# A fused cross-attention and FFN kernel: later FFN weight loads, a new order on every engine, filler products in the fill, rope pairs in fours

## The reference

```python
x = x + xattn(layernorm(x), ctx, pos)        # x: 16 batches x 128 tokens x 256
x = x + ffn(layernorm(x))
# xattn: q = x@Wq, k, v = split(ctx@Wkv); 32 heads of 8 values
#   rope on q and k: per head 2 positions x 2 frequencies x (x1, x2)
#   out = (x1*cos - x2*sin, x1*sin + x2*cos)
#   softmax(q k^T / sqrt(8)) v, then @Wout + bout
# ffn: 4-bit fake-quantised x, W1 (1024x256), W2 (256x1024); relu, h clipped to 0..15
#   the weight scale is max|W| / 7, so W1 and W2 are needed whole before they are rounded
```

## Time and profile before

| what | value |
|---|---|
| median of 3 runs | 263.78 us (262.29 to 264.59) |
| the profiled execution, its own time | 261.2 us |
| its span, first to last instruction | 259.2 us |
| PE busy | 219.5 us (85%) |
| DVE busy | 202.3 us (78%) |
| ACT busy | 183.8 us (71%) |
| POOL busy | 145.2 us (56%) |
| DMA | 11.28 MB, mean 44 GB/s |

### The profile page before, as it was taken

The page is one execution under the profiler, slowest core; times in us unless marked ns, Lnnn a source line. Parts: engine busy times, 40 slices in busy tenths (PEclk is TensorE's granted clock), DMA queues, the critical chain, the costliest instruction groups (busy, mean ns, idle before and its releaser), DMA issues.

```text
span 259.2 us, 8209 instructions
## 1 busy us (share of the span) xinstructions
PE 219.5 (85%) x3126; PEld 173.6 (67%) x3126; DVE 202.3 (78%) x418; ACT 183.8 (71%) x346; POOL 145.2 (56%) x232
## 2 busy tenths in 40 slices
PE   0342775897899999999999999999999999899763
PEld 0142663765677878788877887878787778687541
DVE  5188449967559898989898998989898989884641
ACT  2132339675557979788897979797979799788553
POOL 3158747583636675858493949494948381411320
PEclk9999957599689999999999999999999999999985
DMA  7982000029000000100010001000100010010101
GB/s 193 369 243 89 0 3 1 4 51 359 4 4 4 1 4 4 44 6 5 1 46 4 4 5 44 3 4 4 44 4 5 3 46 5 4 44 4 42 0 40
DMA packets 11381, 11.28 MB, mean 44 GB/s; under 512 B 3920, under 2 KB 10576, under 8 KB 11216
## 3 DMA queue, kind: packets, MB, share of 16 engines
q1 hardware_dynamic: 8864, 10.23, 12.1%
q10 hardware_dynamic: 2480, 0.54, 1.0%
HBM read 8.41 MB, written 2.10 MB: 41 GB/s over the span
## 4 chain that ended last, share of the span: by engine, by line
PE 72%; POOL 6%; DVE 6%; DMA 6%; issue 6%; ACT 3%; ACTq 0%; POOLq 0%; DVEq 0%
PE ps_misc L947 43%; PE ps_av L947 14%; PE ps_exp L947 12%; PE ps_max L947 4%; DMA wq<-in_L_xattn_Wq_dram 3%; DMA q_stack<-mxT 3%; ACT h_i L606 2%; POOL rot L444 2%; DVE mx L797 1%; POOL qk_rows L455 1%; POOL xcT_hi L431 1%; POOL v_strip L395 1%; POOL xcT_lo L434 1%; DVE xq_i L854 1%; POOL v_strip L469 1%
## 5 line engine op out<-in xcount | busy, mean ns | idle before, releaser
L797 DVE TENSOR_REDUCE mx<-ps_max 128x8 f32<-128x1024 f32 x64 | 78.0, 1219 | 14.5 <-PE ps_max L947 12.6
L576 ACT ACTIVATE expo<-ps_exp 128x1024 f32<-128x1024 f32 x64 | 68.3, 1068 | 7.9 <-PE ps_exp L947 7.8
L444 POOL TENSOR_TENSOR rot<-by_cos,by_sin 128x256 f32<-128x256 f32 x32 | 26.3, 842 | 54.2 <-DVE by_sin L787 54.2
L606 ACT ACTIVATE h_i<-ps_misc,b1q,relu_scale 128x128 int16<-128x128 f32 x128 | 49.2, 499 | 1.3 <-PE ps_misc L947 1.2
L947 PE MATMUL ps_exp<-q_stack,k_stack 25*128 25x128 f32 x512 | 44.0, 290 | 5.6 <-DMA q_stack<-mxT 3.0
L947 PE MATMUL ps_misc<-ident,qk_rows 128*128 128x128 f32 x256 | 40.0, 293 | 9.0 <-POOL qk_rows L455 9.0
L947 PEld LDWEIGHTS ps_exp<-q_stack,k_stack 25*128 25x128 f32 x512 | 34.9, 191 | 16.9 <-issue 8.7
L947 PE MATMUL ps_av<-expo,v_strip 128*32 128x128 f32 x1024 | 42.3, 285 | 0.0
L947 PEld LDWEIGHTS ps_misc<-ident,qk_rows 128*128 128x128 f32 x256 | 32.0, 152 | 11.0 <-issue 6.0
L947 PEld LDWEIGHTS ps_av<-expo,v_strip 128*32 128x32 f32 x1024 | 24.8, 111 | 6.9 <-issue 0.8
L866 DVE TENSOR_SCALAR hq<-h_i 128x512 bf16<-128x512 int16 x32 | 18.7, 586 | 11.9 <-ACT h_i L606 11.9
(11 more groups left out here) (117 smaller groups left out, 447.7 us busy)
## 6 DMA issues: line engine op xcount, KB each, us to landing
w<-in_L_ffn_W_dram SPq DMA_DIRECT2D x2, 1024.0 KB, 8.1
out_dram<-y SPq DMA_DIRECT2D x8, 256.0 KB, 2.8
xcT<-in_ctx_dram SPq DMA_DIRECT2D x1, 1536.0 KB, 6.5
x_all<-in_x_dram SPq DMA_DIRECT2D x1, 1024.0 KB, 10.5
xcT<-in_ctx_dram SPq DMA_DIRECT2D x1, 768.0 KB, 6.6
x_all<-in_x_dram SPq DMA_DIRECT2D x1, 512.0 KB, 7.6
q_stack<-mxT SPq DMA_DIRECT2D x32, 8.0 KB
xcT<-in_ctx_dram SPq DMA_DIRECT2D x2, 192.0 KB, 3.5
```

Source lines behind the costliest of these rows:

```text
L444: pool.tensor_tensor(out[:, :, c], kept[:, :, c], turned[:, :, 1 - c], ALU.add).then_inc(rot_ready, 1)
L576: act.activation(expo[:, at, :], ps_exp[:, :, :].rearrange("p m t -> p (m t)"), ACT.Exp, scale=SCALE)\
L606: ins = act.activation(h_i[:, r, f, :], ps_misc[PIECE_BANK[(H0, H1)[half]]][:, 128 * c:128 * c + 128], ACT.Relu, bias=b1q[:, f:f + 1], sca ...
L797: dve.tensor_reduce(out=mx[:, r, 8 * unit:8 * unit + 8], in_=ps_max[:, :, :].rearrange("p m (i k) -> p (m i) k", i=4), axis=AX.X, op=ALU.m ...
```

## The change

It moves and adds the following.

- **Loads.** ACT's queue sends Wq first, then positions, then Wkv. SP waits for Wq and Wkv before it sends W1, W2 and all behind them. Batches 8 to 15 are sent in step 3 between the two placements of batch 0.
- **PE.** `keep_busy(8)`: eight products of `ident_bf` with 256 columns into `ps_av`, read by nobody. 16 stand in step 0 ahead of QK, 40 in step 1 ahead of SQ0 (with VV among them) and 8 behind SK0, 32 in step 2. New cyclic order of the groups: MX0 AV1 SC3 WO VV H1 SK1 AV2 SC0 AV3 MX1 YY SQ0 SC1 SQ1 QK AV0 SK0 AT1 XQ SC2 H0 AT2. Before: SK0 XQ SC2 MX0 AT2 H0 AV1 SC3 WO H1 AV2 VV SK1 SC0 AV3 MX1 YY SQ0 SQ1 SC1 QK AV0 AT1. The banks of the groups follow: bank 1 MX0 WO SK1 SQ0 QK XQ, bank 2 VV YY SK0 H0, bank 0 H1 MX1 SQ1 AT1 AT2.
- **DVE**, new order of a step: maxima 1, rope, norm1_stats, normalise, (centre_wq, quantise_weights 0, rope_tables, spread_maxima), maxima 2, copy_maxima 0, norm1_moments, split_attnT, maxima 3, residual, (quantise_weights 1), norm2_stats, (prepare_scales), norm1_variance, norm2_moments and variance, clip_h 0, clip_h 1, (weight_maxima 0), maxima 0, (prepare_levels), copy_maxima 1, (round_b1), quantise_x 0, (round_b2, spread_tables), quantise_x 1, (weight_maxima 1), output. In brackets: in one step of the fill only.
- **ACT**: copy_av, (split_wout), copy_queries 0, (round_weights 0), copy_queries 1, exponentials 1, copy_keys 0, copy_xqT, exponentials 2, (sines), copy_attnT, relu 0, split_high, exponentials 3, relu 1, (round_weights 1), copy_v, copy_keys 1, exponentials 0. Before, both roundings stood together ahead of split_high.
- **POOL**: (split of Wkv), output_bias, scale_table, split_inputs high, (fill_strips, now in step 0), norm2, rotate, residual_bias, split_inputs low, (split of Wq), place_values, split_low, norm. Before, fill_strips closed step 1, and norm2, norm and scale_table stood behind split_low.
- **Rope in fours.** The columns of Wq and Wkv are laid out per head as four x1, then four x2, on the host, and tables and `rotate` follow: POOL reads runs of 4 values where it read every second one.

```diff
@@ SP @@
+                if late.has(S_MAX):
+                    place_maxima(late, 0, S_MAX)
+                if st.s == 3:
+                    load_both(4)
                 if late.has(S_MAX):
                     place_maxima(late, 1, S_MAX)
-                if st.has(S_MAX):
-                    place_maxima(st, 0, S_MAX)
                 if late.has(S_FFN) and late.ring(S_FFN) == 1:
                     store(late)
-                if st.s == 3:
-                    load_both(4)
...
             load_both(1)
+            sp.wait_ge(wq_loaded, 16)
+            sp.wait_ge(wkv_loaded, 16)
             sp.dma_start(w1[:, :, :], w1_d.rearrange("(c p) f -> p c f", p=128)).then_inc(w_loaded, 16)
@@ POOL, rotate @@
-                kept, turned = [t[:, :].rearrange("p (h c) -> p h c", c=2) for t in (by_cos, by_sin)]
+                kept, turned = [t[:, :].rearrange("p (h c f) -> p h c f", c=2, f=4) for t in (by_cos, by_sin)]
...
-                    pool.tensor_tensor(out[:, :, c], kept[:, :, c], turned[:, :, 1 - c], ALU.add).then_inc(rot_ready, 1)
+                    pool.tensor_tensor(out[:, :, c, :], kept[:, :, c, :], turned[:, :, 1 - c, :], ALU.add).then_inc(rot_ready, 1)
@@ ACT @@
+            act.dma_start(wq[:, :, :], wq_d.rearrange("(c p) d -> p c d", p=128)).then_inc(wq_loaded, 16)
             act.dma_start(pos_sb[:, :, :], pos.rearrange("b t p -> t b p")).then_inc(pos_loaded, 16)
-            act.dma_start(wq[:, :, :], wq_d.rearrange("(c p) d -> p c d", p=128)).then_inc(wq_loaded, 16)
@@ PE @@
+            def keep_busy(n):
+
+                pe.wait_ge(id_ready, 4)
+                pe.wait_ge(ident_bf_ready, 1)
+                for _ in range(n):
+                    mm(ps_av[:, 0:256], ident_bf[:, :], ident[:, :].bitcast(BF16))
```

More of the change, by code:

```diff
@@ L39 @@
 STEPS = BATCH + S_FFN + 1
-SK0, XQ, MX0, AT2, H0, WO, H1, VV, SK1, MX1, YY, SQ0, SQ1, QK, AT1 = range(15)
+MX0, WO, VV, H1, SK1, MX1, YY, SQ0, SQ1, QK, SK0, AT1, XQ, H0, AT2 = range(15)
 PIECES = 15
-PIECE_BANK = (2, 1, 1, 0, 2, 1, 0, 2, 1, 0, 2, 1, 0, 1, 0)
+PIECE_BANK = (1, 1, 2, 0, 1, 0, 2, 1, 0, 1, 2, 0, 1, 2, 0)
 UNITS = 4
@@ L496, in body @@
                 later = Step(st.s - 2)
+                if st.s == 0:
+                    split_weight(0, wkv_lo[:, :], wkv[:, :], wkv_hi[:, :].bitcast(F32))
+                if later.has(S_OUT):
+                    output_bias(later)
+                if late.has(S_PROJ):
+                    scale_table(late)
                 if st.has(S_PROJ):
                     split_inputs(st, False)
+                if st.s == 0:
+                    fill_strips()
+                if later.has(S_OUT):
+                    norm2(later)
                 if late.has(S_PROJ):
                     rotate(late)
[L501 to L506, removed]
+                if late.has(S_ATT):
+                    residual_bias(late)
                 if st.has(S_PROJ):
                     split_inputs(st, True)
+                if st.s == 0:
+                    split_weight(1, wq_lo[:, :, :], wq[:, :, :], wq_hi[:, :, :].bitcast(F32))
                 if late.has(S_MAX):
@@ L632, in body @@
                     exponentials(late, 1)
+                if late.has(S_STACK):
+                    copy_keys(late, 0)
+                if late.has(S_FFN):
+                    copy_xqT(late)
+                if late.has(S_ATT):
+                    exponentials(late, 2)
                 if st.s == S_PROJ:
                     take_sines()
[L635 to L642, removed]
                 if late.has(S_OUT):
@@ L885, in body @@
                     rope(late)
+                if st.has(S_PROJ):
+                    norm1_stats(st)
                 if late.has(S_OUT):
                     normalise(late)
+                if st.s == 0:
+                    centre_wq()
+                if late.s == 2:
+                    quantise_weights(0)
+                if st.s == 0:
+                    rope_tables()
+                if st.s == 2:
+                    spread_maxima()
                 if late.has(S_MAX):
@@ L967, in _ @@
                 QK: (rope_terms, S_PROJ, 2, 2),
+                SK0: (k_ready, S_STACK, 2, 1),
                 AT1: (attn_ready, S_OUT, 1, 1),
+                XQ: (xqT_ready, S_FFN, 1, 1),
+                H0: (relu_done, S_FFN, 2, 1),
+                AT2: (attnT_lo_ready, S_OUT, 1, 1),
             }
-            behind = {SK0: 1, XQ: 1, MX0: 1, AT2: 1, H0: 1, WO: 1, H1: 1, VV: 1, SK1: 1, MX1: 1, YY: 1}
+            behind = {MX0: 1, WO: 1, VV: 1, H1: 1, SK1: 1, MX1: 1, YY: 1}
             def claim(st, piece):
@@ L1219, in body @@
                     weigh_values(st, 0)
+                if st.has(S_STACK):
+                    transpose_rows(st, SK0, K_AT, k_in_psum, 0)
                 if st.has(S_OUT):
                     transpose_av(st)
+                if late.s == 0:
+                    keep_busy(8)
+                if st.has(S_FFN):
+                    transpose_xq(st)
+                if st.s == 2:
+                    keep_busy(8)
+                if st.has(S_MAX) or st.has(S_ATT):
+                    scores(st, 2)
+                if st.s == 2:
+                    keep_busy(8)
+                if st.has(S_FFN):
+                    hidden(st, 0, H0)
+                if st.has(S_OUT):
+                    transpose_attn(st)
             centre_sums()
```

133 lines of the change are left out of this document (62 added, 71 removed).

## The result

The changed kernel takes 249.82 us (median of 4 runs, 249.13 to 250.0) where the kernel before took 263.03 (4 runs, 260.13 to 264.59): ratio 0.9554, 95% interval 0.9499 to 0.9609. The span of the profiled execution fell from 259.2 to 248.0. Those are 13.2 us by the medians and 11.2 by the spans; on the chip of experiment 11 the same pair of kernels differs by 10.2, so the gain is 10 to 13 us and the digits behind that depend on which runs of the kernel before are taken. In the experiments, executions more than 1.5% above the fastest of their kernel are left out of medians, ranges and ratios. The page of the changed kernel: span, busy share of PE in 40 slices, granted clock in tenths.

The account below looks back on a forecast made before the run. PE was taken to set the pace, DVE close behind; 9.4 us gained to batch 5, 0.5 lost in steady steps and 0 in the drain give 8.9 off the 263.78 median: 254.9, own range 251.5 to 258, widened to 249 to 261.5.

Parts of the forecast that it names:

- rival 1: The clock holds and the bubbles go: batch 5 at 65.0, cadence down 0.15, 248.8 us in all; chance 0.11.
- Start: Up to rope of batch 0: earlier Wq and Wkv, less 2.4 for the strips, give 16.5, 2.1 earlier.
- Batches 0 to 2: Two fill intervals, 8.8 each (8.1 to 10.0) from 9.66 and 10.32, by rotate and full clock, less filler lateness.
- Batch 2 to 3: Fill interval that DVE carries with quantised weights: 12.5 (12.0 to 13.5), from 13.06.
- Batch 3 to 4: Fill interval changed by little but clock and rotate: 10.3 (9.7 to 10.8), from 10.60.
- Batch 4 to 5: Fill interval where maxima waited behind the 2.5 MB; sent a step earlier, 12.2 (11.0 to 13.5) from 16.25.
- Full steps: Ten steady intervals: cadence 12.55 (12.35 to 12.85) instead of 12.50, 0.5 lost in all.
- The 0.25 bubble of the loop QK to SC3: In full steps, DVE's chain sums to 5.25 against about 5.0 of PE work between, leaving 0.25 idle.
- Rival 4: XQ waits for rope's read-out of shared bank 1; cadence 13.6, 265.9 us, slower than before; chance 0.07.
- the second rival: Both clips of h on DVE lose to POOL at 1.12; cadence 12.85 to 12.9, 258.6 us; chance 0.12.
- Drain: Stages of the last batch after its rope, number and order as before: nothing gained, plus or minus 1.5.
- rival 5: The fillers only delay: no clock gain and 1.5 late in each of two intervals, 258 us; chance 0.05.

Follow-up runs that it names:

- experiment 11: The changed kernel run again, nothing edited, as the measure of the third chip: 249.75 us, ratio 0.961 to the kernel before.
- Experiment 10: The changed kernel with fill_strips back in step 1 and Wkv sent ahead of the positions: 246.46 us, ratio 0.947 to the kernel before.
- experiment 4: The changed kernel with fill_strips back at the end of POOL's step 1: 247.27 us, ratio 0.949 to the kernel before.
- experiment 12: As Experiment 10, with ACT's second rounding of FFN weights moved from behind relu 1 to behind copy_keys 0: 246.66 us, ratio 0.949.
- experiment 3: The changed kernel with batches 8 to 15 sent a step later: 254.58 us, ratio 0.980 to the kernel before.
- experiment 7: The kernel before with batches 8 to 15 sent a step earlier, its only edit: 256.83 us, ratio 0.979.
- experiment 5: The changed kernel with all fill edits taken back, only the new orders of PE, DVE, ACT and POOL left: 258.5 us, ratio 0.988 to the kernel before.
- experiment 9: The changed kernel with rope values in pairs as before: 250.34 us, ratio 0.963 to the kernel before.
- experiment 6: The kernel before with fillers, loads as changed and rope in fours, old orders, strips in step 1: 248.31 us, ratio 0.948.
- experiment 8: The kernel before with the fillers alone, in the old order: 258.39 us, ratio 0.989.
- experiment 1: The changed kernel without its 96 filler products: 251.98 us, ratio 0.968 to the kernel before.

## Why the prediction was right, point by point

The forecast held: 254.9 said, 249.0 to 261.5 the range, 249.82 measured, at its lower edge. The forecast's own range, 251.5 to 258, was missed; the wider one was let down to 249 for rival 1, whose path came in half (the cadence fell by 0.11, of its 0.15; batch 5 was at 70.11, not 65.0). The sum was 8.9, the span gave 11.2 and the medians 13.2.

Of the 5.1 us between 254.9 and 249.82, 2.6 come from the base: the forecast for the execution profiled was 252.3, and 2.6 were added because the median before lay that much above it. The changed kernel's execution, 249.89, lies on its median, so that addition was wrong. Most of the rest is in the span, 2.3: the start gained 1.3 less than said, rope of batch 0 to 5 took 52.26 instead of 52.6, full steps gained 1.66 more and the drain 1.64 more. The fill as a whole fits by luck, since its parts are off by -0.1, -0.8, +1.1, +0.2 and -0.7.

- **Start** (16.5 said, 17.85 measured, for a gain of 2.1 that was 0.77). The chain from Wkv to QK came out as summed, 7.62 (7.91 to 15.53) for 7.7. The term that was off is the landing of Wkv: 6.5 estimated, 7.91 measured. Experiment 10 shows what lay between: with the positions behind it Wkv is used at 5.88. The cost of the strips was said as 2.4: rows give 2.38 (10.88 to 13.26), experiment 4 gives 2.3 at rope and 2.5 in the median. That W1 and W2 come late did no harm: no wait on them shows in the changed kernel.
- **Batches 0 to 2** (8.8 twice; 8.70 and 8.03). The clock gain in step 1, by the pace of its rows, was had in full. The prediction reads 1.2 and 2.4 GHz off these paces; the granted clock of the kernel before does not bear that out there (1.00 at the slow pace). The doubt about the fillers was justified in kind: 24 of them and SQ0 and SQ1 follow without an idle bracket (SQ0 at 23.91), where low parts end at 23.07 (POOL's row at 21.80, 1.27 long). So they delay SQ0 by 0.8, of the 1.0 that the prediction allowed, and still gain. The second interval is under its range, which began at 8.1.
- **Batch 2 to 3** (12.5, range 12.0 to 13.5; 13.56). The step that failed: a faster chain on POOL and PE was to meet DVE's own sum, and PE's chain ended last instead. DVE is busy only 11.65 of the interval, where it was busy 12.50 of 13.06. The wait that ends last is 0.67 for QK (the bracket at 48.14), at a granted clock of 0.51 from 44.00 to 48.14; without it the interval would be 12.89. The wait of 0.74 for the second rounding, which the prediction named and did not price, is not what the interval lost: without it, in experiment 12, DVE was no further.
- **Batch 3 to 4** (10.3; 10.48) held.
- **Batch 4 to 5** (12.2; 11.49). The mechanism held and is the largest term, 4.76; experiments 3 and 7 show it from both sides, 4.8 and 4.9 us of the medians. It took more than the stall alone: 2.28.
- **Full steps** (12.55; 12.39). Wrong in sign, 0.5 lost against 1.16 gained. The 0.25 bubble of the loop QK to SC3 is not there: the loop takes 4.97 (105.93 to 110.90), where 5.25 was summed and the old order took 5.07. I had 0.95 for normalise; rows 117.22 to 118.32 are 1.10 with 0.20 of waiting for PE in it, so 0.90, and it takes 0.80. From the maxima to SC3 I had 1.40, which in the old order had PE's own queue in it, and it takes 1.29. Rival 4's tie is there and costs nothing that shows: XQ starts at 108.61, 2.68 behind QK, as by_sin ends. That explains why nothing was lost. The 0.11 gained belongs to the orders, as all ten profiled executions with the new ones, experiments 5 and 9 too, go at 12.39 apart from single steps, and all four with the old ones at 12.50; which groups give it is open. By the starts of PE's groups, H0, AT2 and MX0 take 0.88 together instead of 0.98, and no other group differs by more than 0.06. Rows of DVE in a full step after, and PE's SC3:

```profile
108.81 0.36 DVE L819 RECIPROCAL r_sum<-ps_misc 128x36 f32<-128x36 f32 x1
...
109.61 1.22 DVE L801 TENSOR_REDUCE mx<-ps_max 128x8 f32<-128x1024 f32 x1
...
114.05 0.63 DVE L870 TENSOR_SCALAR hq<-h_i 128x512 bf16<-128x512 int16 x1
...
115.52 0.42 DVE L870 TENSOR_SCALAR hq<-h_i 128x512 bf16<-128x512 int16 x1 [0.84 <-ACT h_i L608]
...
110.90 0.32 PE L951 MATMUL ps_exp<-q_stack,k_stack 25*128 25x128 f32 x1
```

- **The clips** of h cost 0.63 and 0.42 a step where they cost 1.12 and 0.29. Both meet POOL now, so the second rival had its premise and not its price. POOL's rows beside them:

```profile
113.25 1.28 POOL L457 TENSOR_TENSOR qk_rows<-rot,qk_rows 128x512 f32<-128x512 f32 x1 [0.56 <-ACT qk_rows L552]
...
115.06 0.73 POOL L494 TENSOR_TENSOR x_b<-x,b2q 128x256 f32<-128x256 f32 x1
```

The first clip ends at 114.68 and POOL's row at 114.53; the second at 115.94, POOL's at 115.79; in the kernel before the long clip ends at 123.74 and POOL's at 123.59. All three are 0.15 behind POOL's end, so the price of a clip was what was left of POOL's instruction when the clip began, and the rival had both at 1.12. DVE is busy 10.88 a step instead of 11.48; the clips are 0.36 of that.
- **Drain** (0; 1.64). Not in the sum: the drain was said to be as before, plus or minus 1.5. The last output lies 50.99 behind the last rope on DVE where it lay 52.64. In the ten profiled executions with the new orders it is 50.57 to 51.90, in the four with the old ones 51.82 to 53.37. So most of it goes with the orders; what in them does it was not looked for.
- **Which edits carry it.** Taken out of the changed kernel one by one (medians against 249.82 and 249.75; only fours was taken out on a chip that also ran the changed kernel), the 2.5 MB a step earlier is worth 4.8, the wait on SP 2.4, the fillers 2.2, fours 0.6 (not clear of noise), the strips in step 0 -2.5. Experiments 5 and 6 bound the orders: 1.2% alone, nothing measurable in the whole with the fill edits there, though full step and drain are shorter. What Wq ahead of the positions gives was not tried alone.
- Two prices of rivals were off by their own terms. Rivals 2 and 4 count the 0.5 of the steady steps twice (258.2 and 265.4 would follow), and rival 5 keeps part of the clock gain that it says is lost (about 260).
- The rivals of the slower side did not come: in the profiled execution no wait over 0.7 on a placement (1.04 once in experiment 11's) and no full step above 12.40.

## What to carry to other kernels

Look for the small transfer that stands in the queue behind a large one, and move the large one to where the next small one is far off: one line gave 4.9 us here, twice the stall it removed. Ask of work moved into the start whether it stands on the chain that sets the first product; 2.4 us of memsets ate most of what earlier weights gave. When a loop is walked, take durations and not distances between starts, or the waits and the queue of the old order are counted again in the new one. A wait that a trace shows is worth its length only if what stands behind it can use the time: the 0.74 of experiment 12 went into a longer instruction.

## What the runs showed of the hardware that was not expected

TensorE can be fully busy and stay at the lower clock for long. In experiment 8 the windows from 47.85 to 62.52 have PE busy 14.63 of 14.67 us:

```profile
47.85:52.00 4.15, 4.15 (x53) 2.73 (x45) 2.38 (x4) 1.73 (x3) 2.79 (x4) 0.50 0.00 0
52.00:56.00 4.00, 3.96 (x43) 2.99 (x39) 2.11 (x6) 2.21 (x3) 3.00 (x7) 0.50 0.48 140
56.00:62.52 6.52, 6.52 (x71) 5.38 (x74) 2.62 (x4) 4.28 (x6) 0.77 (x1) 0.61 0.86 320
```

The granted clock is 0.50, so 1.2 GHz, for the first 8 us and rises only in the third stretch. The kernel before, with the same order, takes 10.60 for this interval at a granted clock of 0.95, the changed kernel 10.48. In experiment 6 the same interval took 15.64, all of it at 0.50, with the DMA at 0.01, so the transfer in the rows above is not needed for it. How busy PE was in batch 2 to 3 does not sort them: 9.62 of 13.06 in the kernel before, which got the full clock back, 8.96 of 12.94 in experiment 8 and 10.31 of 12.94 in experiment 6, which did not. What decides it is open.

The times of these kernels spread, by 2.6 to 5.7 us over all executions of experiments 3, 5, 6, 7 and 8, where the changed kernel has 0.9 and 1.7 on its two chips. That the clock in steps 3 and 4 makes that spread is argued, not shown. For it: in experiment 7 the execution of 254.99 has a mean granted clock of 0.961 and that of 257.63 has 0.939. Against it: in experiment 8 those of 256.41 and 260.04 have 0.942 and 0.943, and the one with the windows above is the faster.

The page shows PE as busy all the while, so a digit of 9 there says nothing without the line of the clock below it. And that line has a gap in the first 28 us: the kernel before (24.00 to 28.28) and experiment 1 (18.31 to 27.58) read 1.00 where eight transposes take 1.94 instead of 1.04. There the durations of like rows are the better witness.
